# First attention of a two-layer gated Flamingo stack: the scaling of the first chunk's keys moves behind the slot's first mask and maximum on VectorE

## The reference, cut to what matters

```python
x = x + tanh(g_xattn[0]) * L0_xattn(layernorm(x), ctx, ctx)      # 16 heads of 32, softmax over 375, causal mask
x = x + tanh(g_ffn[0])   * L0_ffn(layernorm(x), ...)              # Hadamard rotations, 512 -> 2048 -> 512
x = x + tanh(g_xattn[1]) * L1_xattn(layernorm(x), ctx, Wq, Wk, Wv, Wo, q_norm_w, k_norm_w)
x = x + tanh(g_ffn[1])   * L1_ffn(layernorm(x), ...)

# inside L0_xattn, for each of 16 heads
scores = q @ k.T / sqrt(32)
scores = where(ki <= qi + (375 - 112), scores, -10000.)
out = softmax(scores) @ v

# inside L1_xattn: what the first attention of the kernel prepares ahead
k = (ctx @ Wk).reshape(B, 375, 4, 128)
v = (ctx @ Wv).reshape(B, 375, 4, 128)
k = k_norm_w * (k * rsqrt(mean(k * k, -1) + 1e-6))
```

## Time and profile before

| | us |
|---|---|
| median of 3 runs | 2183.25 (2183.11 to 2185.81) |
| the profiled execution, its own time | 2183.04 |
| its span, first to last instruction | 2181.3 |
| mean granted TensorE clock | 0.971 |
| TensorE matmul busy | 2042.6 (94%) |
| TensorE weight load busy | 1691.5 (78%) |
| VectorE busy | 1316.7 (60%) |
| ScalarE busy | 1139.9 (52%) |
| GpSimd busy | 666.3 (31%) |

### The profile page before, as it was taken

How to read it: one execution, slowest core, us unless ns; L and a number is a source line. 1 busy time by engine, 2 the same in 40 slices (tenths; PEclk the granted TensorE clock), 3 DMA queues, 4 the chain that set the end, 5 groups by cost and what they waited for, 6 DMA issues and landing times. The chain is left out here.

```text
span 2181.3 us, 38580 instructions
## 1 busy us (share of the span) xinstructions
PE 2042.6 (94%) x13464; PEld 1691.5 (78%) x13464; DVE 1316.7 (60%) x2603; ACT 1139.9 (52%) x3025; POOL 666.3 (31%) x814
## 2 busy tenths in 40 slices
PE   5999999999989999999969995999999999689997
PEld 4777777777768888898848884888888888578884
DVE  5666667666644543564345554777777776466664
ACT  4666666666643333443323435677667665245453
POOL 2424425345311000000014443554555554012221
PEclk9999999999999999999979997999999999799997
DMA  5435436344265210100033344322322320311010
GB/s 151 151 97 151 146 96 212 117 145 136 92 201 191 76 58 1 68 4 27 0 121 116 116 120 137 100 71 98 103 92 72 107 98 13 109 50 43 28 34 26
DMA packets 167398, 205.96 MB, mean 94 GB/s; under 512 B 63680, under 2 KB 105664, under 8 KB 166752
## 3 DMA queue, kind: packets, MB, share of 16 engines
q1 hardware_dynamic: 167264, 204.15, 29.8%
HBM read 128.13 MB, written 75.99 MB: 94 GB/s over the span
## 5 line engine op out<-in xcount | busy, mean ns | idle before, releaser
L1729 POOL TENSOR_TENSOR c_probs<-c_probs,c_rsum 112x375 f32<-112x375 f32 x256 | 213.1, 835 | 231.1 <-DVE c_rsum L1839 225.3
L1835 DVE TENSOR_REDUCE c_nmax<-c_score 112x1 f32<-112x375 f32 x256 | 136.2, 533 | 97.4 <-PE c_score L1905 97.4
L1783 ACT ACTIVATE c_pT_hi<-c_turned 125x336 fp32r<-125x336 f32 x256 | 115.6, 452 | 107.9 <-PE c_turned L1913 107.9
L1224 ACT ACTIVATE b_silu<-b_gate,b_ug_scale 128x512 f32<-128x512 f32 (+1 forms) x64 | 40.7, 636 | 250.1 <-PE b_up L1330 250.0
L1281 DVE SCALAR_TENSOR_TENSOR b_hidden<-b_up,b_ug_scale,b_silu 128x512 f32<-128x512 f32 (+1 forms) x64 | 43.7, 683 | 204.8 <-ACT b_silu L1224 204.8
L547 ACT ACTIVATE a_probs<-a_score,a_nmax 112x375 f32<-112x375 f32 x256 | 144.7, 576 | 36.5 <-DVE a_nmax L707 36.5
L1776 ACT ACTIVATE c_probs<-c_score,c_nmax 112x375 f32<-112x375 f32 x256 | 148.2, 579 | 0.0
L918 PEld LDWEIGHTS a_turned<-keep_ident,a_probs 112*125 112x125 f32 x768 | 110.6, 189 | 47.0 <-issue 34.7
L918 PE MATMUL a_turned<-keep_ident,a_probs 112*125 112x112 f32 x768 | 135.1, 285 | 9.6 <-DVE a_pT L713 9.6
L1454 POOL TENSOR_TENSOR q_x_ve<-q_x_mv,keep_ln_eps 128x1 f32<-128x1 f32 x14 | 2.7, 192 | 444.8 <-DVE q_x_mv L1531 444.8
L2108 POOL TENSOR_TENSOR f_probs<-f_probs,f_rsum 112x448 f32<-112x448 f32 x64 | 60.3, 942 | 243.8 <-DVE f_rsum L2228 243.5
(11 more groups left out here) (306 smaller groups left out, 5986.7 us busy)
## 6 DMA issues: line engine op xcount, KB each, us to landing
q<-q_qT SPq DMA_DIRECT2D x14, 1024.0 KB
c_q_raw<-q SPq DMA_DIRECT2D x16, 896.0 KB
k<-ab_stage SPq DMA_DIRECT2D x16, 752.0 KB, 4.3
c_k_raw<-k SPq DMA_DIRECT2D x16, 752.0 KB
v<-ab_stage SPq DMA_DIRECT2D x48, 250.0 KB
c_v_raw<-v SPq DMA_DIRECT2D x16, 750.0 KB
ab_lead<-in_ctx_dram SPq DMA_DIRECT2D x16, 672.0 KB
wug<-a_ug_turned SPq DMA_DIRECT2D x32, 256.0 KB, 2.4
```

What stands on the lines that cost most here:

```text
L1729: pool.tensor_tensor(probs[:, h % AHEAD, :], probs[:, h % AHEAD, :], rsum[:, p, h:h + 1].broadcast_to([S, T]), ALU.mult).then_inc(scaled, 1)
L1783: act.activation(pT[0][:, g % 2, :, j, :], src, ACT.Copy).then_inc(pT_hi, 1)
L1835: dve.tensor_reduce(nmax[:, p, h:h + 1], score[h % AHEAD][0:S, 0:T], axis=AX.X, op=ALU.max, negate=True).then_inc(max_done, 1)
```

## The change

In slot 2, VectorE's `scale_keys(b, 0)` is issued behind the slot's first `maximum` (`maximum(b, 4)`) instead of ahead of it. It stays ahead of `probs_copy(b, 2)`. The scaling of the second and third chunk stays where it was, and no other engine's list changes.

```diff
@@ -768,8 +768,6 @@
                 for n in range(PAIRS):
                     if n == 0 and before:
                         scale_keys(b - 1, 2)
-                    if n == 2 and cur:
-                        scale_keys(b, 0)
                     if n == 3 and after:
                         ctx_lo(b + 1, 1)
                     if n == 5 and after:
@@ -781,6 +779,8 @@
                             maximum(b, n + 2)
                         elif after:
                             maximum(b + 1, n + 2 - PAIRS)
+                    if n == 2 and cur:
+                        scale_keys(b, 0)
                     if n == 0 and before:
                         reciprocals(b - 1)
                     if n == 1 and before:
```

## The result

| | before | after |
|---|---|---|
| median, us | 2183.59 (2183.11 to 2185.81, 4 runs) | 2168.14 (2167.1 to 2169.78, 4 runs) |
| profiled execution, us | 2183.04 | 2167.37 |
| span, us | 2181.3 | 2165.7 |

The ratio is 0.9928 with a 95% interval of 0.9911 to 0.9945: faster by 15.4 us (0.7%), where 23.7 was forecast. The time lies 1.6 us above the range.

What follows compares the result with a forecast made beforehand. TensorE was taken to bound the first attention, with two stops a batch; 14 x 1.55 + 2.00 = 23.7 us off the profiled 2183.04 gives 2159.3, plus 0.21 for the median 2159.5 us; range 2153.5 to 2166.5, 88%.

Steps and rivals of the forecast that it cites:

- What bounds the kernel: First attention: runs at TensorE's pace, matmuls busy 94% of the span, plus two small stops a batch.
- TensorE's two stops a batch: Waits for VectorE's transpose copy (9.0 us) and ScalarE's values' copy (11.6 us), both from VectorE idling ahead of the scaling.
- The moved scaling costs nothing: VectorE, slot 2: scaling still starts at 187.20, as VectorE is free 0.31 us before the root is there.
- Gain of 1.55 us up to slot 3: TensorE, fifth batch: next context transpose starts at 189.50 in place of 191.05; the same taken for 14 batches.
- The recorded idle time: TensorE's waits in the rows, 11.6 + 9.0 = 20.6 us, taken as the lower bound of the gain, giving 2162.7.
- What is late next: Transpose of the scaled keys would come at 191.67; the low part of the context allows 191.56, 0.11 us to spare.
- The rival "something else binds a little earlier": Low part of the context or values' copy 0.2 us later: gain 1.35 a batch, about 2162.6 us; 13%.
- The clock: Rival: the granted clock's fall after the first batch's stops, 42.4 to 46.0 us, vanishes, worth 1.7 us: 2157.8; 15%.
- The whole sum: First attention: 14 x 1.55 + 2.00 = 23.7 us gained, everything behind it starting that much earlier.
- The first batch: TensorE's transpose starts at 39.39 instead of 41.39, a gain of 2.00 us.

Runs made afterwards that it cites:

- e9_add_later: Against the changed kernel: a one-column GpSimd instruction added ahead of its first addition in the 8 batches that have additions; 2160.54 us.
- e3_before_norm_late: Against the kernel before, without the swap: next batch's normalising moved from slot 2 to the end of VectorE's list for slot 3; 2182.62 us.
- e4_quiet_only: Against the kernel before: the swap made only in the 8 batches without GpSimd additions in slot 2; 2171.9 us.
- e1_norm_late: Against the changed kernel: next batch's normalising moved from slot 2 to the end of VectorE's list for slot 3; 2159.62 us.
- e6_one_add: Against the changed kernel: GpSimd's second addition moved behind its work on the second chunk's keys, leaving one in slot 2; 2158.56 us.
- e8_norm_mid: Against the changed kernel: the normalising put ahead of slot 2's second maximum in VectorE's list; 2160.43 us.

## Why the prediction was wrong

- **What bounds the kernel: right.** TensorE's two stops a batch were real, had one cause, and in all 15 batches neither is recorded any more.
- **The moved scaling costs nothing: right.** VectorE stands 0.21 us ahead of it in the fifth batch, 0.31 was worked out.
- **Gain of 1.55 us up to slot 3: right**, to 0.01 us, in both kinds of batch. The recorded idle time (0.57 + 0.77 us) was indeed the poorer measure.
- **What is late next: wrong, and this is the step that failed.** I named the right instruction, the transpose of the keys behind the low part, with 0.11 us to spare. But I moved the normalising as a block of fixed length, "from the copy at 187.81, with 192.04 - 189.09 = 2.95 us between". 1.34 us was not its length but the distance to 0.3 us behind the end of GpSimd's additions. Those hang on GpSimd's root and do not move up with VectorE. At 189.50 the normalising meets the start of the second addition (about 189.5 by the profile), and if that one goes first, must end 0.3 us behind 191.84 as before. Worked out so, the low part comes at 192.04 + 0.66 = 192.70, TensorE at 192.84 instead of 193.22, and the gain is 0.38 in these batches; 0.3 was measured. The sum would have been 7 x 1.55 + 8 x 0.38 = 13.9 us, or 2169.4. The rows for it stood there: 1.34 beside the additions, 0.54 without. Which of the two goes first at 189.50 no row of the kernel before tells; e9_add_later, where the normalising comes 0.13 us earlier against the first addition's end than in the changed kernel, shows it going first.
- **The rival "something else binds a little earlier"** had this place and this cause, but was given 0.2 us, for the same reason; in 8 batches it was 1.25.
- **The clock: it came out as the rival says, but the reason is not shown.** In the changed kernel no fall of the granted clock stands behind the first batch's slot 3. Yet e3_before_norm_late and e4_quiet_only, with the first batch's stops as in the kernel before, have none either. Their stretches that answer to the earlier trace rows, with 1.00 as the granted clock:

```profile
42.40:46.00 3.60, 3.60 (x22) 2.92 (x21) 1.82 (x4) 2.17 (x6) 0.00 (x0) 1.00 0.24 72
42.40:46.00 3.60, 3.60 (x29) 2.96 (x31) 1.52 (x3) 2.00 (x7) 0.00 (x0) 1.00 0.41 121
```

So the same stops stand once with the fall and twice without it, and its absence needs no swap; whether the swap makes it rarer is open. The first batch's scores of slots 2 and 4 lie 12.81 us apart with the fall and 11.22 and 11.19 without it: 1.6 us, where 1.7 was worked out. They are part of the 15.6 us between the spans of the two profiled executions.
- **How near the time came is in part luck.** From first to last scores the gain is 7 x 1.55 + 8 x 0.3 = 13.3 us of the swap and 1.6 us of the clock, together the measured 14.9. The hold took 10 us off the forecast 23.7, and the missing fall gave 1.6 back.
- **The whole sum, without the hold, was right:** 23.7 us forecast; by medians in the same runs 24.1 us in e1_norm_late and 25.1 in e6_one_add. From first to last scores they are 25.2 and 25.3 us shorter, which is the 23.7 and the clock's 1.6. The first batch, forecast at 2.00 us, gives 11.19 - 9.24 = 1.95.

## What to carry to other kernels

When a change lets an engine reach an instruction earlier, ask of each instruction behind it whether its duration is its own work or ends with something else; an instruction with two durations in one trace (0.54 and 1.34 us here) is the sign, and its end belongs in the sum, not its length. A normalising from SBUF to SBUF on VectorE beside long GpSimd additions should stand where nothing urgent is behind it in the list; here that one line's place was worth 8.5 us by medians (10.3 us of the first attention), and only once the stop that covered it was gone.

## What the runs showed of the hardware

- A `tensor_scalar` of 112 x 512 from SBUF to SBUF takes 0.54 us alone and ends 0.3 us behind the GpSimd addition that holds it: 1.34, 1.59 and 2.67 us in three orders of the same work. It holds GpSimd too (an addition of 2.39 us became 2.56 to 2.68 in e8_norm_mid and e9_add_later).
- Between two GpSimd instructions in a row VectorE gets its turn if its instruction starts early enough, by the profile: 0.16 us ahead of the first one's end it had its turn (seven times), at 0.15 us (once) and at 0.02 to 0.04 us (eight times, in the changed kernel) it was passed by.
- The same instruction over views of step 2 keeps its speed and its hold (0.54 and 2.66 us).
